# Cutting the mixed columns at 0, 136 and 648: one bank to route by, two of output

## The chip, the cores and the metric

The kernel runs on one core of a Trainium2 chip. The metric is the device time in microseconds, the median of several executions. A core has a matrix engine (TensorE, PE in the rows; its weight loads are listed apart as PEld), a vector engine (VectorE, DVE), a scalar engine (ScalarE, ACT), GpSimd (POOL), and queues that issue transfers (SyncE, SP). Matrix products land in PSUM, which has eight banks of 512 fp32 columns per partition.

## The reference, cut to what matters

Shapes: x is 128 samples of 64 channels by 1024; the output has the same shape.

```
h     = gelu(gelu(cond @ W0 + b0) @ W1 + b1)
att   = softmax(h @ W2 + b2)                              # 8 kernels per sample
y     = einsum('boi,bih->boh', att-weighted kernels, x) + bias   # mixes the 64 channels
logits= y @ W_router.T                                    # 8 experts
w     = top 2 of softmax(logits), renormalized
h_e   = einsum('nd,erd->ner', y, A)                       # rank 16, 8 experts
out   = x + y @ W_base.T + b_base + 2 * einsum('ner,eor->no', h_e * w, B)
```

## The kernel before, in words

Mixing the channels and multiplying by the wide matrix commute, so the kernel first multiplies the raw x by one matrix of 1160 columns, in this order: 128 columns of `A` (experts by rank), 8 of the router (together `AR` = 136), and 1024 of `W_base`. It calls the product z. Then it mixes: a 128x128 matrix that holds two samples' channel mixers is multiplied with z. The first 136 mixed columns are what a token is routed by; the other 1024 are output.

Rows come in 64 tiles of 128 (two samples each), two tiles to a unit, 32 units. The large product of a unit is a 2x2 block product done in seven products instead of eight (`A11`, `A12`, `S2`, `S1`, `S3`, `S4`, `A22`, where the S are sums of blocks that VectorE makes). Each product is made of matmuls of 290 columns, in two parts of twelve. fp32 accuracy comes from a split into a high and a low fp32r part: every product is three matmuls, high by high, high by low and low by high. ScalarE makes the high part by a cast, VectorE the low part by a subtraction, and so for x, for z (four blocks: z11 and z12 of the unit's first tile, z21 and z22 of the second), for the mixers and for the routed rows.

Behind the product each tile has two passes on TensorE:

- the mixed pass (`mixed`, lines 474 to 504): 3 pieces of columns, cut by `CUTS` at 0, 384 and 772, three matmuls each, into banks 4, 5 and 6. Piece 0 holds the 136 columns to route by and the first 248 of the output; its last matmul releases the routing on VectorE (`route`). Piece 1 first waits for the low part of z12 (or z22) and for `rest_put`.
- the experts' pass (`experts`, lines 506 to 518): the weighted, transposed rows `hwT` (high and low) by `b_hi` and `b_lo`, added to the output columns that stand in the same banks. With the cuts as they are that is 248, 388 and 388 columns, three times.

Then VectorE adds the tile's banks to `x_sb`, which already holds bias and x (`result`, two instructions), and SyncE stores it. Before the next tile's mixed pass ScalarE writes the tile's column bias into the banks (`seed`: piece 0 when `head_out` says that VectorE has read it, pieces 1 and 2 on `out_done`), so that the mixed pass accumulates on it.

The order of the work on each engine is written out by hand in `unit`, once per engine, with semaphores between. For unit u TensorE does: A11, A12, S2, experts of tile (u-1, 0), S1, mixed of (u-1, 1), S3, S4, experts of (u-1, 1), A22, mixed of (u, 0). VectorE's order in unit 1 is apart (`unit_1`); the last unit is written out too, with `expert_piece` and `add_piece` per piece and the last tile's stores cut in two.

Of the kernel before, what the change touches and what calls it, by code (L numbers as in the profile page):

```python
# [23 lines left out]
BANK = 512  # L24
# [5 lines left out]
XBLOCK = CHUNKS * P  # L30
WBLOCK = CHUNKS * HALF

CUTS = (0, 384, 772, WIDE)
PIECES = 3
LORA_SCALE = 2.0
ROUTE_STEPS = 9

# [58 lines left out]

def out_columns(piece):

    first = max(CUTS[piece], AR)
    return slice(first - AR, CUTS[piece + 1] - AR), slice(first - CUTS[piece], CUTS[piece + 1] - CUTS[piece])  # L100


def build(nc, x, xT, small, keep, mix_w, wide, b_base, bT, out):
# [8 lines left out]
    with ExitStack() as ctx:  # L112
# [117 lines left out]
        tile_bias_done = sem("tile_bias_done")  # L230
        head_put = sem("head_put")
        rest_put = sem("rest_put")
        head_out = sem("head_out")
        mix_hi_done = sem("mix_hi_done")
        mix_lo_done = sem("mix_lo_done")
        product_mm = sem("product_mm")
# [115 lines left out]
        @block.sync  # L352
        def _(sp):
            def load_mix(u, side):
                pair = agg_w_pairs[tile_no(u, side)]
                for par in range(PAIR):
                    blk = slice(par * CH, (par + 1) * CH)
                    sp.dma_start(mix[blk, side, blk], pair[blk, :]).then_inc(mix_in[side], 16)

            def load_first_mix(side):  # L360
                for par in range(PAIR):
                    b, blk = side * PAIR + par, slice(par * CH, (par + 1) * CH)
                    sp.dma_start(mix[blk, side, blk], agg_w[b:b + 1, :].rearrange("b (i o) -> b i o", i=CH)
                                 ).then_inc(mix_in[side], 16)

            def load_xT(u):
                sp.dma_start(xT_sb[:].rearrange("p b n -> p (b n)"), xT_units[u]).then_inc(xT_in, 16)

            def store(u, side):
                sp.wait_ge(out_done, tile_no(u, side) + 1)  # L370
                sp.dma_start(out_tiles[tile_no(u, side)], x_sb[:, side, :]).then_inc(stored[side], 16)

            def load_first(name):
                at = RAW[name]
                sp.dma_start(xT_sb[:, at, :], xT_units[0][:, at * XBLOCK:(at + 1) * XBLOCK]  # L375
                             ).then_inc(first_xT_in[at], 16)

            load_first("A11")
            for c in range(CHUNKS):
                cols = slice(c * HALF, (c + 1) * HALF)  # L380
                sp.dma_start(w_stage[:, 0, cols], wide_blocks[0][:, cols]).then_inc(b11_in[c], 16)  # L381
            load_first("A21")
            sp.dma_start(small_sb[:], small).then_inc(small_in, 16)
            load_first("A12")
            for h, js in enumerate(HALVES):
                cols = slice(js.start * HALF, js.stop * HALF)
                sp.dma_start(w_stage[:, 1, cols], wide_blocks[2][:, cols]).then_inc(b21_in[h], 16)
            load_first("A22")
            for h, js in enumerate(HALVES):
                cols = slice(js.start * HALF, js.stop * HALF)  # L390
                sp.dma_start(b12_sb[:, cols], wide_blocks[1][:, cols]).then_inc(b12_in[h], 16)
            for h, js in enumerate(HALVES):
                cols = slice(js.start * HALF, js.stop * HALF)
                sp.dma_start(b22_sb[:, cols], wide_blocks[3][:, cols]).then_inc(b22_in[h], 16)
            sp.wait_ge(x_lo_done, FIRST_SPLITS)
            load_xT(1)
            sp.wait_ge(zeroed, 2)
            sp.wait_ge(agg_done, 2 * GROUPS)
            load_first_mix(0)
            load_first_mix(1)  # L400
            sp.dma_start(agg_w_dram.rearrange("(b i) o -> b (i o)", b=BATCH), agg_w[:]).then_inc(agg_w_out, 16)
            sp.dma_start(bias_out[:], b_base.partition_broadcast(P)).then_inc(bias_out_in, 16)
            for side in range(2):
                sp.wait_ge(mix_in[side], 16 * PAIR)
            sp.wait_ge(agg_w_out, 16)
            sp.dma_start(bT_stage, bT).then_inc(bT_in, 16)
            sp.wait_ge(mix_lo_done, 2)
            load_mix(1, 0)
            load_mix(1, 1)

            def unit(u, par, first=False, early=False):
                store(u - 1, 0)
                sp.wait_ge(mix_lo_done, tile_no(u, 0) + 1)
                load_mix(u + 1, 0)
                sp.wait_ge(x_lo_done, splits(u, "A22"))
                load_xT(u + 1)
                store(u - 1, 1)
                sp.wait_ge(mix_lo_done, tile_no(u, 1) + 1)
                load_mix(u + 1, 1)

            units(sp, unit)
            store(LAST - 1, 0)
            store(LAST - 1, 1)
            sp.wait_ge(out_done, tile_no(LAST, 0) + 1)
            sp.dma_start(out_tiles[tile_no(LAST, 0)], last_x[:, 0, :]).then_inc(stored[0], 16)
            last_cols = [slice(0, out_columns(1)[0].stop), out_columns(2)[0]]
            for n, cols in enumerate(last_cols):
                sp.wait_ge(out_done, tile_no(LAST, 1) + 1 + n)
                sp.dma_start(out_tiles[tile_no(LAST, 1)][:, cols], last_x[:, 1, cols]).then_inc(stored[1], 16)
            sp.wait_ge(stored[0], UNITS * 16)  # L430
            sp.wait_ge(stored[1], UNITS * 16 + 16)

        @block.tensor
        def _(pe):
# [69 lines left out]
                mixed(1, 2, start=not seeded).then_inc(mixed_mm, 1)  # L504

            def expert_part(stat, mov, banks):
                for k in range(PIECES):
                    res, at = out_columns(k)
                    mm = nc.tensor.matmul(ps[:, banks[k], at], stat[:], mov[:, res], start=False, stop=True,  # L509
                                          skip_group_check=True)  # L510
                return mm

# [6 lines left out]

            def expert_piece(side, k, bank, start=False):  # L520

                res, at = out_columns(k)
                dst = ps[:, bank, at]
                pe.wait_ge(hwT_hi_done, tile_no(LAST, side) + 1)
                nc.tensor.matmul(dst, hwT_hi[:], b_hi[:, res], start=start, stop=False, skip_group_check=True)
                nc.tensor.matmul(dst, hwT_hi[:], b_lo[:, res], start=False, stop=False, skip_group_check=True)
                pe.wait_ge(hwT_lo_done, tile_no(LAST, side) + 1)
                return nc.tensor.matmul(dst, hwT_lo[:], b_hi[:, res], start=False, stop=True, skip_group_check=True)
# [172 lines left out]
                product_part(b, "S4", part, False).then_inc(last_half_mm, 1)  # L701
            pe.wait_ge(z22_lo_done, u + 1)
            mixed(1, 1, LAST_BANKS[1], last_z_hi, last_z_lo)
            expert_piece(0, 0, O_BANKS[0]).then_inc(last_piece_mm, 1)
            expert_piece(0, 1, O_BANKS[1], True)
            expert_piece(0, 2, O_BANKS[2], True)
            pe.wait_ge(last_half_summed, 1)
# [3 lines left out]
            mixed(0, 1, start=False).then_inc(last_piece_mm, 1)  # L711
            pe.wait_ge(last_half_lo_done, 2)
            mixed(0, 2, start=False).then_inc(last_piece_mm, 1)
            for k in range(PIECES):
                expert_piece(1, k, LAST_BANKS[k]).then_inc(last_piece_mm, 1)

        @block.scalar
        def _(act):
# [31 lines left out]
            def seed(u, side):  # L750

                t = tile_no(u, side)
                act.wait_ge(tile_bias_done, t - 1)
                act.wait_ge(head_out, t)
                nc.scalar.activation(ps[:, O_BANK, 0:width(0)], col_sum[:, columns(0)], ACT.Copy,
                                     scale=tile_bias[:, side:side + 1]).then_inc(head_put, 1)
                act.wait_ge(out_done, t)
# [261 lines left out]
        def _(dve):  # L1019
# [93 lines left out]
            def result(u, side):  # L1113
                t = tile_no(u, side)
                dve.wait_ge(x_in[side], u * 16 + 16)
                dve.wait_ge(out_mm, t + 1)
                res, at = out_columns(0)
                nc.vector.tensor_tensor(x_sb[:, side, res], ps[:, O_BANK, at], x_sb[:, side, res], ALU.add
                                        ).then_inc(head_out, 1)
                rest = x_sb[:, side, res.stop:D].rearrange("p (k n) -> p k n", k=2)  # L1120
                nc.vector.tensor_tensor(rest, ps[:, O_BANK + 1:O_BANK + 3, out_columns(1)[1]], rest,  # L1121
                                        ALU.add).then_inc(out_done, 1)

            def put_biases(u, side, place=x_sb):

# [71 lines left out]
            def unit_1():  # L1197
# [30 lines left out]
                dve.wait_ge(product_mm, products(1, "S4"))  # L1228
                add_acc(sum2, b, z12_summed)
                result(0, 1)  # L1230
                make_s3(2)
                x_low(2, "A11")
                z12_low(1)
                x_low(2, "A12")
                dve.wait_ge(x_lo_done, splits(2, "A11"))
                make_s2(2)
# [99 lines left out]
            hwT_low(u, 1)  # L1336

            def add_piece(side, k, bank):
                dve.wait_ge(last_piece_mm, side * PIECES + k + 1)
                res, at = out_columns(k)  # L1340
                return nc.vector.tensor_tensor(last_x[:, side, res], ps[:, bank, at], last_x[:, side, res], ALU.add)  # L1341

            dve.wait_ge(x_in[0], u * 16 + 16)
            add_piece(0, 0, O_BANKS[0])
            add_piece(0, 1, O_BANKS[1])
            add_piece(0, 2, O_BANKS[2]).then_inc(out_done, 1)
            dve.wait_ge(x_in[1], u * 16 + 16)
            add_piece(1, 0, LAST_BANKS[0])
            add_piece(1, 1, LAST_BANKS[1]).then_inc(out_done, 1)
            add_piece(1, 2, LAST_BANKS[2]).then_inc(out_done, 1)  # L1350

# [45 lines left out]
```

## Time and profile before

| what | value |
|---|---|
| median of 3 runs | 944.49 us (944.46 to 944.65) |
| the profiled execution | 944.94 us |
| its span, first to last instruction | 943.3 us |
| TensorE busy | 936.6 us, 99% |
| VectorE busy | 773.8 us, 82% |
| ScalarE busy | 476.4 us, 51% |
| granted TensorE clock | 1.00 of full speed |

The span lies inside the execution's own time, which is 1.64 us longer. A matmul's duration in the rows is from its start to its modelled end and overlaps that of the next one; what a matmul costs in a full queue is the distance between the starts of two neighbours. Rows of the timeline merge neighbouring instructions of one kind (x3), and then give the time from the first start to the last end.

### The profile page before, as it was taken

Reading aid. Unit: us, or ns where it says so; the run is one execution under the profiler, and the core shown is the slowest. Engines: PE = TensorE matmul, PEld = TensorE weight load, DVE = VectorE, ACT = ScalarE, POOL = GpSimd, SP = SyncE. Lnnn points to the kernel's source line nnn. Section 1 sums busy time; section 2 is a strip of 40 time slices with the busy share of each in tenths; the row PEclk is TensorE's granted clock in tenths of the full one; section 3 lists DMA queues with packets and bytes.
Section 4 is the critical chain, followed back from the end, with each engine's and each line's share of the span. In section 5 each row is a group of like instructions: output and inputs, shape, how many; then the busy total and the mean of one; then the engine's idle time right before and its main releaser. Section 6 shows DMA issues by size and latency. Waiting matters only on the chain.

```text
span 943.3 us, 19762 instructions
## 1 busy us (share of the span) xinstructions
PE 936.6 (99%) x6687; PEld 932.7 (99%) x6687; DVE 773.8 (82%) x2327; ACT 476.4 (51%) x915; POOL 97.5 (10%) x139
## 2 busy tenths in 40 slices
PE   9999999999999999999999999999999999999998
PEld 8999999999999999999999999999999999999997
DVE  5986666888888888888888888888888888888876
ACT  6655454545454455454454555454545454545451
POOL 1130101100101100101010101001011001011010
PEclk9999999999999999999999999999999999999999
DMA  8444435343445343444344354444353434453434
GB/s 300 149 109 103 108 116 137 95 133 90 104 127 134 92 127 79 114 134 115 111 112 92 114 136 105 122 95 110 114 136 97 129 91 107 120 136 93 134 91 112
DMA packets 36055, 111.41 MB, mean 118 GB/s; under 512 B 13200, under 2 KB 13456, under 8 KB 31936
## 3 DMA queue, kind: packets, MB, share of 16 engines
q1 hardware_dynamic: 26656, 77.32, 22.5%
q0 software_dynamic: 9376, 33.78, 21.9%
q8 instruction: 14, 0.23, 0.1%
q14 instruction: 9, 0.07, 0.0%
HBM read 75.37 MB, written 35.65 MB: 118 GB/s over the span
## 4 chain that ended last, share of the span: by engine, by line
PE 97%; DMA 1%; DVE 1%; SPq 0%; issue 0%; ACT 0%; DVEq 0%
PE ps L446 25%; PE ps L444 25%; PE ps L442 25%; PE ps L509 9%; PE ps L478 4%; PE ps L476 4%; PE ps L480 4%; DMA w_stage<-in_wide 1%; PE ps L469 0%; PE ps L468 0%; PE ps L535 0%; DVE w_stage L1341 0%; SPq L381 0%; SPq L375 0%; DVE w_lo L1133 0%
## 5 line engine op out<-in xcount | busy, mean ns | idle before, releaser
L442 PE MATMUL ps<-w_hi,x_hi 128*128 128x290 f32 x1544 | 457.9, 297 | 0.4 <-DVE x_lo L1138 0.3
L446 PE MATMUL ps<-w_hi,x_lo 128*128 128x290 f32 x1544 | 458.0, 297 | 0.0
L444 PE MATMUL ps<-w_lo,x_hi 128*128 128x290 f32 x1544 | 457.8, 296 | 0.0
L442 PEld LDWEIGHTS ps<-w_hi,x_hi 128*128 128x128 f32 x1544 | 292.0, 189 | 2.4 <-DVE w_lo L1133 0.9
L444 PEld LDWEIGHTS ps<-w_lo,x_hi 128*128 128x128 f32 x1544 | 291.4, 189 | 0.0
L446 PEld LDWEIGHTS ps<-w_hi,x_lo 128*128 128x128 f32 x1544 | 291.1, 189 | 0.0
L1107 DVE STREAM_TRANSPOSE blocks_hwT<-hw 32x32 f32<-32x32 f32 x832 | 168.5, 203 | 25.3
L720 ACT CAST x_hi<-xT_sb 128x512 fp32r<-128x512 f32 x186 | 112.5, 620 | 29.9 <-DVE xT_sb L1038 22.2
L1022 DVE TENSOR_TENSOR x_lo<-xT_sb,x_hi 128x512 fp32r<-128x512 f32 x186 | 125.1, 686 | 0.7 <-ACT x_hi L720 0.7
L763 ACT COPY sum<-ps 128x580 f32<-128x580 f32 x96 | 62.0, 646 | 111.4 <-PE ps L446 111.4
L993 POOL DMA_DIRECT2D x_sb<-in_x x62 | 53.7, 867 | 510.5 <-ACT x_sb L744 495.0
L739 ACT CAST hwT_hi<-blocks_hwT 128x128 fp32r<-128x128 f32 x52 | 15.6, 299 | 144.7 <-DVE blocks_hwT L1107 144.7
L988 POOL TENSOR_TENSOR mix_lo<-mix,mix_hi 128x128 fp32r<-128x128 f32 x64 | 47.7, 746 | 302.8 <-ACT mix_hi L724 302.8
L1041 DVE TENSOR_TENSOR sum<-ps,sum 128x580 f32<-128x580 f32 x91 | 68.8, 756 | 7.5 <-PE ps L446 7.4
L446 PE MATMUL ps<-t_hi,x_lo 128*128 128x290 f32 x248 | 74.2, 299 | 0.0
L442 PE MATMUL ps<-t_hi,x_hi 128*128 128x290 f32 x248 | 74.2, 299 | 0.0
L444 PE MATMUL ps<-t_lo,x_hi 128*128 128x290 f32 x248 | 73.9, 298 | 0.0
L476 PE MATMUL ps<-z_hi,mix_hi 128*128 128x384 f32 x189 | 64.0, 339 | 0.3 <-DVE z_lo L1050 0.3
L478 PE MATMUL ps<-z_hi,mix_lo 128*128 128x384 f32 x189 | 63.9, 338 | 0.0
L480 PE MATMUL ps<-z_lo,mix_hi 128*128 128x384 f32 x189 | 63.8, 338 | 0.0
L744 ACT COPY x_sb<-bias_out 128x1024 f32<-128x1024 f32 x60 | 62.8, 1046 | 0.0
L1121 DVE TENSOR_TENSOR x_sb<-ps,x_sb 128x776 f32<-128x776 f32 x62 | 59.2, 956 | 0.0
(137 smaller groups left out, 1232.3 us busy)
## 6 DMA issues: line engine op xcount, KB each, us to landing
xT_sb<-in_xT SPq DMA_DIRECT2D x31, 1024.0 KB, 4.9
x_sb<-in_x POOLq DMA_DIRECT2D x62, 512.0 KB, 5.4
result<-x_sb SPq DMA_DIRECT2D x62, 512.0 KB, 2.7
b_sb<-in_wide SPq DMA_DIRECT2D x4, 580.0 KB, 13.6
agg_w_rows<-agg_w SPq DMA_DIRECT2D x1, 2048.0 KB, 7.5
mix<-agg_w_rows SPq DMA_DIRECT2D x124, 16.0 KB, 2.5
w_stage<-in_wide SPq DMA_DIRECT2D x4, 290.0 KB, 5.3
w_stage<-in_wide SPq DMA_DIRECT2D x2, 580.0 KB, 8.3
```

The lines of the kernel that those rows point to most:

```text
L442: nc.tensor.matmul(dst, x_hi[:, s, rows], high[:, c, cols], start=first, stop=False, skip_group_check=True)
L444: nc.tensor.matmul(dst, x_hi[:, s, rows], low[:, c, cols], start=False, stop=False, skip_group_check=True)
L446: mm = nc.tensor.matmul(dst, x_lo[:, s, rows], high[:, c, cols], start=False, stop=last, skip_group_check=True)
L476: nc.tensor.matmul(dst, mix_hi[:, side, :], high[:, columns(k)], start=start, stop=False, skip_group_check=True)
L478: nc.tensor.matmul(dst, mix_lo[:, side, :], high[:, columns(k)], start=False, stop=False, skip_group_check=True)
L480: return nc.tensor.matmul(dst, mix_hi[:, side, :], low[:, columns(k)], start=False, stop=True, skip_group_check=True)
L509: mm = nc.tensor.matmul(ps[:, banks[k], at], stat[:], mov[:, res], start=False, stop=True, skip_group_check=True)
L720: nc.scalar.copy(x_hi[:, SLOT[name], :], raw(name)).then_inc(x_hi_done, 1)
L744: nc.scalar.copy(x_sb[:, side, :], bias_out[:]).then_inc(out_bias_put, 1)
L1022: nc.vector.tensor_tensor(x_lo[:, SLOT[name], :], raw(name), x_hi[:, SLOT[name], :].bitcast(F32), ALU.subtract).then_inc(x_lo_done, 1)
L1041: nc.vector.tensor_tensor(dst[:], acc(first), dst[:], ALU.add).then_inc(done, 1)
L1107: nc.vector.transpose(blocks_hwT[there, here], hw[here, there]).then_inc(blocks_made, 1)
```

## The change: new cuts, two output pieces

The cuts move from 0, 384, 772 to 0, 136, 648. Piece 0 is then exactly the 136 columns to route by; pieces 1 and 2 are a full bank of output each. The experts' pass touches only pieces 1 and 2, with 512 columns each. `result` becomes one instruction over both banks, and the semaphore `head_out` goes: the seed of piece 0 waits for `hw_done` (the routing has read bank 4). In the last unit one `expert_piece` and one addition per tile go, and the last tile is stored as two halves of 512 columns. In unit 1, `z12_low` moves up by two places on VectorE.

```diff
-CUTS = (0, 384, 772, WIDE)
-PIECES = 3
+CUTS = (0, AR, AR + BANK, WIDE)
+OUT_PIECES = (1, 2)
...
 def out_columns(piece):
-    first = max(CUTS[piece], AR)
-    return slice(first - AR, CUTS[piece + 1] - AR), slice(first - CUTS[piece], CUTS[piece + 1] - CUTS[piece])
+    return slice(CUTS[piece] - AR, CUTS[piece + 1] - AR)
...
             def expert_part(stat, mov, banks):
-                for k in range(PIECES):
-                    res, at = out_columns(k)
-                    mm = nc.tensor.matmul(ps[:, banks[k], at], stat[:], mov[:, res], start=False, stop=True,
+                for k in OUT_PIECES:
+                    mm = nc.tensor.matmul(ps[:, banks[k], :], stat[:], mov[:, out_columns(k)], start=False, stop=True,
                                           skip_group_check=True)
...
-            expert_piece(0, 0, O_BANKS[0]).then_inc(last_piece_mm, 1)
             expert_piece(0, 1, O_BANKS[1], True)
...
-            for k in range(PIECES):
+            for k in OUT_PIECES:
                 expert_piece(1, k, LAST_BANKS[k]).then_inc(last_piece_mm, 1)
...
                 act.wait_ge(tile_bias_done, t - 1)
-                act.wait_ge(head_out, t)
+                act.wait_ge(hw_done, t)
...
-                nc.vector.tensor_tensor(x_sb[:, side, res], ps[:, O_BANK, at], x_sb[:, side, res], ALU.add
-                                        ).then_inc(head_out, 1)
-                rest = x_sb[:, side, res.stop:D].rearrange("p (k n) -> p k n", k=2)
-                nc.vector.tensor_tensor(rest, ps[:, O_BANK + 1:O_BANK + 3, out_columns(1)[1]], rest,
-                                        ALU.add).then_inc(out_done, 1)
+                out = x_sb[:, side, :].rearrange("p (k n) -> p k n", k=2)
+                nc.vector.tensor_tensor(out, ps[:, O_BANK + 1:O_BANK + 3, :], out, ALU.add).then_inc(out_done, 1)
...
                 result(0, 1)
+                z12_low(1)
                 make_s3(2)
                 x_low(2, "A11")
-                z12_low(1)
                 x_low(2, "A12")
...
-            add_piece(0, 0, O_BANKS[0])
             add_piece(0, 1, O_BANKS[1])
...
-            add_piece(1, 0, LAST_BANKS[0])
             add_piece(1, 1, LAST_BANKS[1]).then_inc(out_done, 1)
```

TensorE's mixed pass of a tile stood before as follows (`z_hi`, `z_lo` the split product, `mix_hi`, `mix_lo` the split mixer):

```order
L476 MATMUL ps<-z_hi,mix_hi 128x384
L478 MATMUL ps<-z_hi,mix_lo 128x384
L480 MATMUL ps<-z_lo,mix_hi 128x384
L476 MATMUL ps<-z_hi,mix_hi 128x388
L478 MATMUL ps<-z_hi,mix_lo 128x388
L480 MATMUL ps<-z_lo,mix_hi 128x388
```

and stands now:

```order
L475 MATMUL ps<-z_hi,mix_hi 128x136
L477 MATMUL ps<-z_hi,mix_lo 128x136
L479 MATMUL ps<-z_lo,mix_hi 128x136
L475 MATMUL ps<-z_hi,mix_hi 128x512
L477 MATMUL ps<-z_hi,mix_lo 128x512
L479 MATMUL ps<-z_lo,mix_hi 128x512
```

Three more like the last three follow in each. The number of matmuls is the same, nine, and their columns add up to the same 1160.

The experts' pass, also on TensorE, behind product S2 (and again behind S4), before:

```order
L509 MATMUL ps<-b_hi,hwT_hi 128x248
L509 MATMUL ps<-b_hi,hwT_hi 128x388 x2
L509 MATMUL ps<-b_lo,hwT_hi 128x248
L509 MATMUL ps<-b_lo,hwT_hi 128x388 x2
L509 MATMUL ps<-b_hi,hwT_lo 128x248
L509 MATMUL ps<-b_hi,hwT_lo 128x388 x2
```

and now:

```order
L445 MATMUL ps<-w_hi,x_lo 128x290
L507 MATMUL ps<-b_hi,hwT_hi 128x512 x2
L507 MATMUL ps<-b_lo,hwT_hi 128x512 x2
L507 MATMUL ps<-b_hi,hwT_lo 128x512 x2
L441 MATMUL ps<-w_hi,x_hi 128x290
```

Nine matmuls have become six, over the same columns.

VectorE at the end of unit 1, from the sum that completes z12 on (`sum`; `x_sb<-ps` is `result`, `z_lo<-sum` the low part of z12, the rest makes the next unit's x blocks), before:

```order
L1041 TENSOR_TENSOR sum<-ps,sum 128x580
L1118 TENSOR_TENSOR x_sb<-ps,x_sb 128x248
L1121 TENSOR_TENSOR x_sb<-ps,x_sb 128x776
L1030 TENSOR_TENSOR xT_sb<-xT_sb 128x512
L1022 TENSOR_TENSOR x_lo<-xT_sb,x_hi 128x512
L1050 TENSOR_TENSOR z_lo<-sum,z_hi 128x580
```

and now:

```order
L1038 TENSOR_TENSOR sum<-ps,sum 128x580
L1115 TENSOR_TENSOR x_sb<-ps,x_sb 128x1024
L1047 TENSOR_TENSOR z_lo<-sum,z_hi 128x580
L1027 TENSOR_TENSOR xT_sb<-xT_sb 128x512
L1019 TENSOR_TENSOR x_lo<-xT_sb,x_hi 128x512 x2
```

The z12 split has moved ahead of S3 and of the low part of `A11`, in this unit alone; the merged `result` is in every unit.

## Rows read from the trace of the kernel before

**Rows 1.** The page, its busy times, granted clock and chain of waits.
```profile
PE 936.6 (99%) x6687; PEld 932.7 (99%) x6687; DVE 773.8 (82%) x2327; ACT 476.4 (51%) x915; POOL 97.5 (10%) x139
...
PEclk9999999999999999999999999999999999999999
...
PE 97%; DMA 1%; DVE 1%; SPq 0%; issue 0%; ACT 0%; DVEq 0%
```

**Rows 2.** Waits of TensorE: who waited for whom, total us, times, longest.
```profile
PE ps L476 <- DVE z_lo L1050: 0.3, 1, 0.3
```

**Rows 3.** Timeline of PE, 500 to 506 us: start us, us, engine, line, operation.
```profile
499.97 0.64 PE L509 MATMUL ps<-b_hi,hwT_hi 128*128 128x248 f32 x3
...
501.37 0.30 PE L442 MATMUL ps<-w_hi,x_hi 128*128 128x290 f32 x1
...
503.00 0.30 PE L442 MATMUL ps<-w_hi,x_hi 128*128 128x290 f32 x1
...
504.21 0.29 PE L442 MATMUL ps<-w_hi,x_hi 128*128 128x290 f32 x1
...
504.61 0.34 PE L476 MATMUL ps<-z_hi,mix_hi 128*128 128x384 f32 x1
...
505.13 0.34 PE L476 MATMUL ps<-z_hi,mix_hi 128*128 128x388 f32 x1
...
506.02 0.33 PE L480 MATMUL ps<-z_lo,mix_hi 128*128 128x388 f32 x1
506.19 0.30 PE L442 MATMUL ps<-w_hi,x_hi 128*128 128x290 f32 x1
```

**Rows 4.** Timeline of PE, 15 to 16 us: two matmuls of 8 columns.
```profile
15.29 0.28 PE L535 MATMUL ps<-small_sb,h2T 128*128 128x8 f32 x2
```

**Rows 5.** The same two by line: durations in ns, min/median/max.
```profile
L535 PE MATMUL ps<-small_sb,h2T x2: 172/214/256, 15.3 to 15.3; 128*128 128x8 f32 x2
```

**Rows 6.** Timeline of PEld, 15.4 to 15.85 us.
```profile
15.67 0.19 PEld L442 LDWEIGHTS ps<-w_hi,x_hi 128*128 128x128 f32 x1 [0.19 <-DVE w_lo L1133]
15.78 0.19 PEld L444 LDWEIGHTS ps<-w_lo,x_hi 128*128 128x128 f32 x1
```

**Rows 7.** Timeline of PE, 53 to 54 us.
```profile
53.43 0.27 PE L532 MATMUL ps<-keep_sb,hw 128*128 128x128 f32 x1
...
53.67 0.30 PE L444 MATMUL ps<-w_lo,x_hi 128*128 128x290 f32 x1
```

**Rows 8.** Timeline of all engines in unit 1, 75.9 to 77.1 us.
```profile
75.93 0.77 DVE L1050 TENSOR_TENSOR z_lo<-sum,z_hi 128x580 fp32r<-128x580 f32 x1
...
76.11 0.34 PE L480 MATMUL ps<-z_lo,mix_hi 128*128 128x384 f32 x1
...
76.74 0.19 PEld L476 LDWEIGHTS ps<-z_hi,mix_hi 128*128 128x128 f32 x1 [0.61 <-DVE z_lo L1050]
...
77.03 0.34 PE L478 MATMUL ps<-z_hi,mix_lo 128*128 128x388 f32 x1
```

**Rows 9.** Timeline of all engines, 501.5 to 505.2 us.
```profile
501.64 0.42 DVE L1118 TENSOR_TENSOR x_sb<-ps,x_sb 128x248 f32<-128x248 f32 x1 [0.47 <-PE ps L509]
...
501.97 0.96 DVE L1121 TENSOR_TENSOR x_sb<-ps,x_sb 128x776 f32<-128x776 f32 x1
...
502.84 0.68 DVE L1030 TENSOR_TENSOR xT_sb<-xT_sb 128x512 f32<-128x512 f32 x1
502.96 0.91 ACT L758 ACTIVATE ps<-col_sum,tile_bias 128x776 f32<-128x776 f32 x1
...
504.04 0.76 DVE L1050 TENSOR_TENSOR z_lo<-sum,z_hi 128x580 fp32r<-128x580 f32 x1
...
504.96 0.19 PEld L476 LDWEIGHTS ps<-z_hi,mix_hi 128*128 128x128 f32 x1
```

**Rows 10.** Line 1341, the last additions: ns min/median/max.
```profile
L1341 DVE TENSOR_TENSOR w_stage<-ps,w_stage x6: 406/553/553, 936.9 to 938.9; 128x388 f32<-128x388 f32 x4, 128x248 f32<-128x248 f32 x2
```

**Rows 11.** DMA issues, 936 to 943.5 us: KB each, us to landing.
```profile
result<-w_stage SPq DMA_DIRECT2D x1, 194.0 KB, 3.3
```

More of the change, by code:

```diff
@@ L232, in build @@
         rest_put = sem("rest_put")
-        head_out = sem("head_out")
         mix_hi_done = sem("mix_hi_done")
@@ L425, in _ @@
             sp.dma_start(out_tiles[tile_no(LAST, 0)], last_x[:, 0, :]).then_inc(stored[0], 16)
-            last_cols = [slice(0, out_columns(1)[0].stop), out_columns(2)[0]]
-            for n, cols in enumerate(last_cols):
+            for n, k in enumerate(OUT_PIECES):
+                cols = out_columns(k)
                 sp.wait_ge(out_done, tile_no(LAST, 1) + 1 + n)
@@ L520, in expert_piece @@
             def expert_piece(side, k, bank, start=False):
-                res, at = out_columns(k)
-                dst = ps[:, bank, at]
+                res = out_columns(k)
+                dst = ps[:, bank, :]
                 pe.wait_ge(hwT_hi_done, tile_no(LAST, side) + 1)
@@ L1116, in result @@
                 dve.wait_ge(out_mm, t + 1)
-                res, at = out_columns(0)
-                nc.vector.tensor_tensor(x_sb[:, side, res], ps[:, O_BANK, at], x_sb[:, side, res], ALU.add
-                                        ).then_inc(head_out, 1)
-                rest = x_sb[:, side, res.stop:D].rearrange("p (k n) -> p k n", k=2)
-                nc.vector.tensor_tensor(rest, ps[:, O_BANK + 1:O_BANK + 3, out_columns(1)[1]], rest,
-                                        ALU.add).then_inc(out_done, 1)
+                out = x_sb[:, side, :].rearrange("p (k n) -> p k n", k=2)
+                nc.vector.tensor_tensor(out, ps[:, O_BANK + 1:O_BANK + 3, :], out, ALU.add).then_inc(out_done, 1)
             def put_biases(u, side, place=x_sb):
@@ L1338, in add_piece @@
             def add_piece(side, k, bank):
-                dve.wait_ge(last_piece_mm, side * PIECES + k + 1)
-                res, at = out_columns(k)
-                return nc.vector.tensor_tensor(last_x[:, side, res], ps[:, bank, at], last_x[:, side, res], ALU.add)
+                dve.wait_ge(last_piece_mm, side * len(OUT_PIECES) + k)
+                res = out_columns(k)
+                return nc.vector.tensor_tensor(last_x[:, side, res], ps[:, bank, :], last_x[:, side, res], ALU.add)
             dve.wait_ge(x_in[0], u * 16 + 16)
-            add_piece(0, 0, O_BANKS[0])
             add_piece(0, 1, O_BANKS[1])
```

## The prediction

> **What bounds the kernel now.** I read the page first. TensorE is busy 99% of the span, the chain of waits runs through it for 97%, and its granted clock is full throughout, the level of 2.4 GHz [rows 1]. Then the waits of TensorE: beyond the start there is one, 0.3 us, on a z split of line 1050 [rows 2]. So every nanosecond that a matmul takes in a full queue is paid, and what VectorE and ScalarE save is worth nothing unless TensorE waits. The timeline then gives what a matmul costs, as the distance between starts [rows 3]:
>
> - 290 columns: nine from 503.00 to 504.21, 0.134 us each.
> - 388 columns: five from 505.13 to 506.02, 0.178 us each.
> - a whole mixed pass: 504.61 to 506.19, about 1.585 us with the rounding (1.58 to 1.59).
> - a whole experts' pass: 499.97 to 501.37, 1.40 us. Six matmuls of 388 are 1.07 of it, which leaves 0.11 for one of 248.
>
> **What a matmul of 136 columns costs.** Nothing in the trace has this shape in a full queue, and the change hangs on it: 192 matmuls (3 in each of 64 tiles) will have it. From 290 to 388 columns the cost grows by 0.044 us for 98, so by columns alone 136 would take 0.134 - 154 x 0.00044 = 0.067 us. But each matmul has its own load of 128x128 weights, and three places show what a load costs when nothing hides it.
>
> - Two matmuls of 8 columns take 0.28 us from the first start to the last end [rows 4]; the shorter, which is the first, takes 172 ns [rows 5]. Their own work is the same, so the second ends 0.11 us behind the first, for 8 columns: it had to wait for its weights.
> - A fresh load of a block of x (fp32r, as the weights here are), the queue empty before it, starts at 15.67, and the next load, which starts when the matmul of the first does, at 15.78: 0.11 us [rows 6].
> - A transposition of 128 columns and the matmul of 290 behind it take 53.43 to 53.67, 0.24 us [rows 7]; less the usual 0.134 that is 0.11 for the 128.
>
> The load of the next matmul runs under the present one, and only that one. A matmul of 248 columns or more covers it; one of 136 can't. I take 0.112 us, bounds 0.108 and 0.114 (the 248 columns' share, which may itself be the load).
>
> The Trainium skill gives for the same thing, in "TensorE: Matmul & The Clock Gate", section "Back-to-back issue gap", about 81 ns for N=128 in a stream of loads and matmuls, and about 131 ns for N=512. The trace speaks against the second figure: 388 columns already take 0.178. By the first the 192 matmuls would cost 192 x 0.031 = 6.0 us less than in my sum, an outcome of its own below.
>
> **What a matmul of 512 columns costs.** From 388 on, at one column per cycle of 2.4 GHz: 0.178 + 124/2400 = 0.229. With the slope between 290 and 388 it is 0.178 + 0.055 = 0.232. I take 0.230; lower end 0.228, upper 0.232.
>
> **The sum, part by part.**
>
> 1. Mixed pass: 3 x 0.112 + 6 x 0.230 = 1.716 against 1.585, +0.131 per tile, 64 tiles: +8.4 us. Three matmuls fall from 0.173 to 0.112 (504.61 to 505.13 was 0.52 for three), not to the 0.067 of their columns, while the six others pay for all the columns moved to them.
> 2. Experts' pass: 6 x 0.230 = 1.38 against 1.40, -0.02 per tile: -1.3 us. Three matmuls fewer, but the same columns, and it is the columns that were paid.
> 3. Unit 1: from 76.11 to 77.03 are 0.92 us, where two matmuls take 0.35 [rows 8]: 0.57 us of stall, a late split and the uncovered load behind it. Moved up two instructions of VectorE, each about 0.60 from start to start, the split ends well before 76.1. What is late next there is the low part of `A11`, made 0.67 later, for a product that starts behind the mixed pass: no wait. -0.6 us.
> 4. `result` as one instruction: before 0.33 + 0.87 = 1.20 us from start to start [rows 9]; by the slope of these two, 0.54 for 528 columns, 1024 take 1.12. VectorE gains 0.08 per tile, worth nothing by itself, but see the second rival.
> 5. Seeds on ScalarE: piece 0 gets shorter and earlier, pieces 1 and 2 go from 776 columns (0.91) to 1024, by columns about 1.1. They start when `result` ends, about 502.9, so end near 504.0, and the mixed matmul that needs them starts after 504.8. Hidden, with 0.7 us to spare. Without this cover each 0.1 us late would cost 6 us over the tiles.
> 6. The tail: what ends last is the last addition and the last store. The addition is of 512 columns instead of 388 (0.553 us [rows 10], by the slope above +0.13), its matmul some 0.05 longer behind its start, and the last store 256 KB instead of 194 [rows 11], of two that hold 512 KB together as before; I put 0.05 on it. +0.2 us. The routing of the last tiles, released 0.18 earlier by the shorter piece 0, isn't what the tail waits for.
>
> Together +8.4 - 1.3 - 0.6 + 0.2 = +6.7 us on the profiled execution's 944.94, so 951.6. The median of the runs before is 0.45 below that execution, and so is the forecast: **951.2 us**. Its own range: the 0.002 on the 12 matmuls of 512 is 1.5 us either way, the bounds of the 136 give -0.8 and +0.4. That is 949.0 to 953.1.
>
> **The rivals.**
>
> - *Columns are all that counts: faster.* The loads are pipelined deeper than one, so 136 columns cost 0.067. For it: a load is listed with 0.19 us [rows 6] and one starts with every matmul, each 0.134, so loads overlap already. Against it: the two matmuls of 8 columns, 0.11 apart. Price: 192 x 0.045 = 8.6 us less, 942.6. It decides from a cost of 0.077 on: below that the pass costs less than it saves. Chance 0.05. The Trainium skill's isolated gap of N/2.4 + 2.5 ns (same page and section as above) is this rule in its purest form; the 290 columns would take 0.123 by it and the trace has 0.134.
> - *A load partly hidden: no change.* The load of the next matmul begins before the present one starts, so that a third of the uncovered 0.045 is left, 0.082 us for a short matmul. For it: nothing but the overlap of the listed loads. Against it: all three places show 0.11. Price: 192 x 0.030 = 5.8 us less than the forecast, 945.4. Chance 0.04. The 81 ns of the Trainium skill, cited above, would be this, and 945.2.
> - *A new wait: slower still.* Piece 1 now comes 3 x 0.112 after the start of the pass instead of 0.52, and its load one matmul earlier, at +0.22 where it was at +0.35 (504.96 against 504.61 [rows 9]). It waits for the z12 split, which ends at 504.80, +0.19, and releases the load some 0.04 later (in unit 1 the split ends at 76.70 and the load starts at 76.74 [rows 8]). With VectorE's 0.08 it is released at about +0.15, so 0.07 to spare. If the merged `result` gains nothing, the two meet; from there every 0.1 us costs 31 x 0.1 = 3.1 us. With 0.1 that makes 954.3. Chance 0.07.
> - *My forecast*, the short matmul bound by its load and no new wait: 0.84.
>
> **How the numbers follow.** The profile bears the forecast's mechanism in three places and no place speaks for less, hence the weight. The range that should hold the time 8 times in 10 is the forecast's own with a little of the third rival: 948.8 to 953.6. A difference of less than 0.2%, 1.9 us, is about what a measurement can't tell from none. Faster takes the first rival, 0.05. The second is no change, 0.04. Slower takes the forecast and the third, 0.91.
>
> **What would show it.** In the profile after, the starts of matmuls of 136 columns lie 0.11 apart and those of 512 columns 0.23; if the first are at 0.07 or 0.08, step 1 is wrong and so is the sign. A mixed pass takes 1.72 us and an experts' pass 1.38. TensorE has no wait on the z12 split, in unit 1 or later; a wait of that name with 30 entries is the third rival. VectorE's busy time falls by about 5 us with no effect. TensorE stays at 99% busy, since a short matmul that waits for its weights is listed as busy.

## The result: 7.1 us slower

| | before | changed |
|---|---|---|
| median, first measurement | 944.57 us (4 runs) | 951.66 us (4 runs, 951.05 to 951.90) |
| span of the profiled execution | 943.3 us | 949.4 us |
| TensorE busy | 936.6 us | 943.8 us |
| matmuls in the trace | 6687 | 6495 |

The ratio is 1.0074, with a 95% interval from 1.0056 to 1.0091. The forecast was 951.2 us, range 948.8 to 953.6.

The page after: TensorE still holds the chain at full clock, with 192 matmuls fewer and 7 us more of busy time; the busy share of its weight loads has fallen [rows 1].

```profile
PE 943.8 (99%) x6495; PEld 907.3 (96%) x6495; DVE 773.0 (81%) x2263; ACT 475.8 (50%) x915; POOL 97.5 (10%) x139
...
PEclk9999999999999999999999999999999999999999
...
PE 98%; DMA 1%; DVE 0%; SPq 0%; ACT 0%; issue 0%; DVEq 0%
```

The timeline of TensorE after, an experts' pass, the product behind it and a mixed pass, the same place in the program as [rows 3]:

```profile
502.80 0.63 PE L507 MATMUL ps<-b_hi,hwT_hi 128*128 128x512 f32 x2
...
504.19 0.29 PE L441 MATMUL ps<-w_hi,x_hi 128*128 128x290 f32 x1
...
507.39 0.23 PE L475 MATMUL ps<-z_hi,mix_hi 128*128 128x136 f32 x1
507.46 0.27 PE L477 MATMUL ps<-z_hi,mix_lo 128*128 128x136 f32 x1
507.57 0.28 PE L479 MATMUL ps<-z_lo,mix_hi 128*128 128x136 f32 x1
507.68 0.44 PE L475 MATMUL ps<-z_hi,mix_hi 128*128 128x512 f32 x1
507.96 0.40 PE L477 MATMUL ps<-z_hi,mix_lo 128*128 128x512 f32 x1
...
508.89 0.39 PE L479 MATMUL ps<-z_lo,mix_hi 128*128 128x512 f32 x1
509.12 0.29 PE L441 MATMUL ps<-w_hi,x_hi 128*128 128x290 f32 x1
```

The mixed pass takes 507.39 to 509.12, 1.73 us, where it took 1.58. Over all passes of the two traces the medians are 1.725 and 1.584. The experts' pass takes 502.80 to 504.19, 1.39, where it took 1.40. A matmul of 512 columns costs (508.89 - 507.96) / 4 = 0.2325 at this place and 1.39 / 6 = 0.232 in the experts' pass. The listed starts of the short matmuls mislead: the second stands 0.07 behind the first, but its duration has grown from 0.23 to 0.27, and the first of the long ones has 0.44 instead of 0.39. So part of a listed duration is waiting. The loads are the better guide: a load starts when the matmul in front of it does, here at 507.39 and again at 507.96. The weight loads at the same place:

```profile
507.39 0.19 PEld L477 LDWEIGHTS ps<-z_hi,mix_lo 128*128 128x128 f32 x1
507.50 0.19 PEld L479 LDWEIGHTS ps<-z_lo,mix_hi 128*128 128x128 f32 x1
507.62 0.19 PEld L475 LDWEIGHTS ps<-z_hi,mix_hi 128*128 128x128 f32 x1
507.73 0.19 PEld L477 LDWEIGHTS ps<-z_hi,mix_lo 128*128 128x128 f32 x1
507.96 0.19 PEld L479 LDWEIGHTS ps<-z_lo,mix_hi 128*128 128x128 f32 x1
```

These are 0.11 us apart for 136 columns, four starts over three matmuls, then 0.23 for 512. The loss grows evenly. The mixed pass of [rows 3] began 2.78 us later after the change (507.39 against 504.61). Thirteen units earlier it began 0.31 us sooner:

```profile
133.49 0.23 PE L475 MATMUL ps<-z_hi,mix_hi 128*128 128x136 f32 x1
```

where the kernel before has

```profile
133.80 0.34 PE L476 MATMUL ps<-z_hi,mix_hi 128*128 128x384 f32 x1
```

That is 3.09 us in 13 units, 0.238 per unit or 0.119 per tile, 7.6 us if it held for all 64.

The early lead has two parts. The first mixed pass of all began 0.41 us sooner in this execution (46.63 against 47.03), before any pass that the change cuts anew; over the fourteen traces of all runs that start lies between 46.55 and 47.27 with no order by kernel, so it is scatter. And the stall of unit 1 [rows 8], 0.57 us, is missing. The two add up to the 1.0 us by which the spans' difference of 6.1 falls short of the medians' 7.1.

### The profile page after: what moved, and what is told of

Its sections match the earlier page's. It is cut to its first block, busy times and chain, and to the rows that moved or that the text cites. A ratio compares the mean times of both kernels' runs of the same rounds, so it can differ in the third digit from the quotient of the medians.

```text
span 949.4 us, 19314 instructions
## 1 busy us (share of the span) xinstructions
PE 943.8 (99%) x6495; PEld 907.3 (96%) x6495; DVE 773.0 (81%) x2263; ACT 475.8 (50%) x915; POOL 97.5 (10%) x139
## 4 chain that ended last, share of the span: by engine, by line
PE 98%; DMA 1%; DVE 0%; SPq 0%; ACT 0%; issue 0%; DVEq 0%
PE ps L445 25%; PE ps L443 25%; PE ps L441 25%; PE ps L507 9%; PE ps L477 4%; PE ps L479 4%; PE ps L475 4%; DMA w_stage<-in_wide 1%; PE ps L468 0%; PE ps L467 0%; DVE w_stage L1334 0%; PE ps L533 0%; SPq L380 0%; SPq L374 0%; DVE w_lo L1126 0%; PE ps L530 0%
## 5 line engine op out<-in xcount | busy, mean ns | idle before, releaser
L1115 DVE TENSOR_TENSOR x_sb<-ps,x_sb 128x1024 f32<-128x1024 f32 x62 | 75.9, 1224 | 32.5 <-PE ps L507 29.9
L755 ACT ACTIVATE ps<-col_sum,tile_bias 128x1024 f32<-128x1024 f32 x60 | 66.9, 1116 | 18.2 <-DVE x_sb L1115 18.2
L477 PE MATMUL ps<-z_hi,mix_lo 128*128 128x136 f32 x189 | 67.3, 356 | 0.0
L479 PE MATMUL ps<-z_lo,mix_hi 128*128 128x136 f32 x189 | 67.1, 355 | 0.0
L475 PE MATMUL ps<-z_hi,mix_hi 128*128 128x136 f32 x189 | 66.8, 353 | 0.0
```

The source lines that it names most:

```text
L475: nc.tensor.matmul(dst, mix_hi[:, side, :], high[:, columns(k)], start=start, stop=False, skip_group_check=True)
L477: nc.tensor.matmul(dst, mix_lo[:, side, :], high[:, columns(k)], start=False, stop=False, skip_group_check=True)
L479: return nc.tensor.matmul(dst, mix_hi[:, side, :], low[:, columns(k)], start=False, stop=True, skip_group_check=True)
L1115: nc.vector.tensor_tensor(out, ps[:, O_BANK + 1:O_BANK + 3, :], out, ALU.add).then_inc(out_done, 1)
```

## The experiments

Twelve further measurements were made, each beside the kernel before on the same chip. Its median differs by up to 0.2 us from one group of runs to the next, so a difference between two rows with another "before there" is uncertain by as much.

| run | median us | before there |
|---|---|---|
| e1 changed kernel again | 951.77 | 944.70 |
| e2 changed, old place of the z12 split | 951.70 | 944.70 |
| e3 changed, piece 0 padded to 248 columns | 952.00 | 944.70 |
| e4 before, z12 split early, store in halves | 943.68 | 944.70 |
| e5 before, z12 split early | 944.45 | 944.52 |
| e6 before, cuts at 264 and 712 | 954.47 | 944.52 |
| e7 changed, `result` in two | 953.09 | 944.52 |
| e8 changed, one load less | 948.30 | 944.52 |
| e9 as e8, z12 split early in every unit | 945.10 | 944.59 |
| e10 as e7, z12 split early in every unit | 951.38 | 944.59 |
| e11 before, last store cut at 624 | 944.15 | 944.59 |
| e12 before, last store in halves | 943.94 | 944.59 |

### Is it the load or the columns?

**e1**, the reference: 

> The changed kernel again, as the reference point for the runs beside it on the same chip. Both theories: 951.7 us, 7.1 above before.

It took 951.77, ratio 1.0075 (1.0061 to 1.0089).

**e3** gives the short matmuls more to do:

```diff
-                dst = ps[:, O_BANK + k if bank is None else bank, 0:width(k)]
+                size = width(k) if k else 248
+                cols = slice(CUTS[k], CUTS[k] + size)
+                dst = ps[:, O_BANK + k if bank is None else bank, 0:size]
```

and `cols` for `columns(k)` in the three matmuls. 

> The changed kernel, but the three matmuls of piece 0 in each mixed pass stream 248 columns instead of 136; the 112 extra columns go into unread places of bank 4. Theory (a short matmul costs its 128x128 weight load, 0.112 us, whatever its columns): 248 columns cost 0.114, so 192 x 0.002 = +0.4 us, 952.1. Rival (columns are what is paid and the loss comes from elsewhere, as from full banks of 512): 112 columns x 0.00044 = 0.049 us each, 192 of them, +9.4 us, 961.

952.00, 0.23 above e1, as the theory has it. The 112 columns more in each of 192 matmuls cost next to nothing. The timeline of TensorE in e3 shows the same spacing, 0.11 to 0.12 us, now with even durations:

```profile
507.75 0.28 PE L477 MATMUL ps<-z_hi,mix_hi 128*128 128x248 f32 x1
507.86 0.28 PE L479 MATMUL ps<-z_hi,mix_lo 128*128 128x248 f32 x1
507.98 0.28 PE L481 MATMUL ps<-z_lo,mix_hi 128*128 128x248 f32 x1
508.09 0.40 PE L477 MATMUL ps<-z_hi,mix_hi 128*128 128x512 f32 x1
```

**e6** puts the short matmul into the other pass, with no matmul of 512 columns in either:

```diff
-CUTS = (0, 384, 772, WIDE)
+CUTS = (0, 264, 712, WIDE)
```

> The kernel before with its cuts at 0, 264 and 712: the mixed pass has pieces of 264, 448 and 448 columns, the experts' pass of 128, 448 and 448. No matmul has 512 columns and the mixed pass has no short one, but the experts' pass has three. Theory (a short matmul costs its load, 0.112): experts 3 x 0.112 + 6 x 0.2045 = 1.563 against 1.404, mixed 3 x 0.123 + 6 x 0.2045 = 1.596 against 1.586, together +0.169 in each of 64 tiles, +10.8 us, 955.3; perhaps 0.2 more for the stall in unit 1. Rival (the loss comes with full banks of 512, columns are what is paid): 128 columns cost 0.063, +0.022 per tile, +1.4 us, 946.

954.47, ratio 1.0108 (1.0092 to 1.0123), 9.95 us above before and 0.8 short of the expected 955.3. The rival's 946 is out. The experts' pass in e6:

```profile
504.12 0.68 PE L509 MATMUL ps<-b_hi,hwT_hi 128*128 128x128 f32 x3
504.64 0.68 PE L509 MATMUL ps<-b_lo,hwT_hi 128*128 128x128 f32 x3
505.16 0.68 PE L509 MATMUL ps<-b_hi,hwT_lo 128*128 128x128 f32 x3
505.68 0.29 PE L442 MATMUL ps<-w_hi,x_hi 128*128 128x290 f32 x1
```

That is 0.52 us for each three and 1.56 at this rounding (1.553 over all such passes), against 1.40: the same 1024 columns three times, 0.15 dearer.

**e8** takes one load away and keeps the columns:

```diff
+                if k == 0:
+                    wide_dst = ps[:, O_BANK if bank is None else bank, 0:2 * AR]
+                    nc.tensor.matmul(wide_dst, mix_hi[:, side, :], high[:, 0:2 * AR], start=start, stop=False,
+                                     skip_group_check=True)
+                    return nc.tensor.matmul(dst, mix_lo[:, side, :], high[:, columns(0)], start=False, stop=True,
+                                            skip_group_check=True)
```

> The changed kernel, but piece 0 of a mixed pass has two matmuls instead of three: mix_hi by 272 columns of z_hi (136 of them into unread places) and mix_lo by 136. The product with z_lo is left out of the columns to route by, as it would be if z_hi and z_lo stood side by side and were streamed as one. The number of columns streamed is the same, 408. Theory (one load fewer that nothing covers): 0.126 + 0.112 = 0.238 against 0.336, -0.098 in 64 tiles, -6.3 us, 945.4. Rival (columns): 0.126 + 0.067 = 0.193 against 0.201, -0.5 us, 951.2.

948.30, 3.5 below e1, between the theory's -6.3 and the rival's -0.5. The timeline of e8 tells why. A mixed pass of a unit's first tile, with the z12 split ahead of it:

```profile
505.02 0.76 DVE L1053 TENSOR_TENSOR z_lo<-sum,z_hi 128x580 fp32r<-128x580 f32 x1
...
505.61 0.29 PE L477 MATMUL ps<-z_hi,mix_hi 128*128 128x272 f32 x1
...
505.74 0.22 PE L479 MATMUL ps<-z_hi,mix_lo 128*128 128x136 f32 x1
505.82 0.19 PEld L481 LDWEIGHTS ps<-z_hi,mix_hi 128*128 128x128 f32 x1
```

and one of a second tile, whose z22 is long split:

```profile
521.59 0.29 PE L477 MATMUL ps<-z_hi,mix_hi 128*128 128x272 f32 x1
...
521.72 0.23 PE L479 MATMUL ps<-z_hi,mix_lo 128*128 128x136 f32 x1
521.72 0.19 PEld L481 LDWEIGHTS ps<-z_hi,mix_hi 128*128 128x128 f32 x1
```

The first load of piece 1 stands 0.21 behind the start of the pass in the one and 0.13 in the other. The split ends at 505.78 and the load follows 0.04 later, as in unit 1 of the kernel before [rows 8]. The pass got so short that the wait of the prediction's third rival came true here, though the list of TensorE's waits shows nothing of it: the matmul in front is listed as busy meanwhile.

**e9** moves the split ahead in every unit:

```diff
                 result(u - 1, 1)
+                z12_low(u)
                 make_s3(u + 1)
                 x_low(u + 1, "A11")
-                z12_low(u)
```

> The kernel with one load less in piece 0 (the product with z_lo left out of the columns to route by), and the z12 split moved ahead of S3 and of the low part of A11 on VectorE in every unit, not in unit 1 alone. Where only one load was taken away the mixed passes took 1.631 us where the split is older, and 1.716 where they wait for z12, 0.085 more. Theory (that difference is the wait for the split, the rest is the load): both kinds take 1.63, -0.085 x 30 = -2.5 us, 945.8. Rival (that difference is not the split): 948.3.

945.10: 3.2 less than e8, and 6.7 below e1. The closest partner is e10 below, which stood beside it, has the early split too and keeps all three matmuls (and has `result` in two, which costs it nothing): 951.38, 6.3 more, which is just what one load of 0.098 in 64 passes gives. That is the third side from which the columns are excluded. Its mixed pass, of a first tile too, takes 504.82 to 506.44, 1.62 us. Against before it is no change that can be told (ratio 1.0007, 0.9997 to 1.0016), and it leaves part of the routing's precision out, so it is no better kernel.

What e3, e6 and e9 exclude is that columns alone are paid. In all of them every matmul brings its own load of 128x128, and none changes the size of a load. A floor of 0.11 us on each pair of load and matmul, from another cause than the weights, would fit them as well; that it is the load itself is argued and not shown.

### How near is the wait for the z12 split?

In the changed kernel the split ends at 507.56, and the load of piece 1 starts 0.06 behind it, at 507.62:

```profile
504.46 1.22 DVE L1115 TENSOR_TENSOR x_sb<-ps,x_sb 128x1024 f32<-128x1024 f32 x1 [0.70 <-PE ps L507]
505.60 0.68 DVE L1027 TENSOR_TENSOR xT_sb<-xT_sb 128x512 f32<-128x512 f32 x1
...
506.80 0.76 DVE L1047 TENSOR_TENSOR z_lo<-sum,z_hi 128x580 fp32r<-128x580 f32 x1
```

**e7** makes VectorE a little slower ahead of the split:

```diff
-                out = x_sb[:, side, :].rearrange("p (k n) -> p k n", k=2)
-                nc.vector.tensor_tensor(out, ps[:, O_BANK + 1:O_BANK + 3, :], out, ALU.add).then_inc(out_done, 1)
+                for k in OUT_PIECES:
+                    cols = out_columns(k)
+                    add = nc.vector.tensor_tensor(x_sb[:, side, cols], ps[:, O_BANK + k, :], x_sb[:, side, cols],
+                                                  ALU.add)
+                add.then_inc(out_done, 1)
```

> The changed kernel with result as two instructions of VectorE again, 512 columns each. Theory (TensorE pays for matmuls and their loads alone; the z12 split is released just in time): VectorE loses about 0.06 us per tile, the split is released at the moment at which the load of piece 1 wants it; 0 to 0.05 us in each of 31 units, 951.7 to 953.2. Rival (the new wait already costs time after the change, so VectorE's time is TensorE's): +0.06 x 31 = +1.9 us or more, 953.6.

953.09, 1.4 us above the changed kernel, at the upper end of the theory. In e7 the split ends at 508.71 and the load starts at 508.76, 0.17 behind the one before it, where the changed kernel has 0.11 to 0.12:

```profile
507.95 0.76 DVE L1047 TENSOR_TENSOR z_lo<-sum,z_hi 128x580 fp32r<-128x580 f32 x1
...
508.59 0.19 PEld L479 LDWEIGHTS ps<-z_lo,mix_hi 128*128 128x128 f32 x1
...
508.76 0.19 PEld L475 LDWEIGHTS ps<-z_hi,mix_hi 128*128 128x128 f32 x1
```

**e10** is e7 with e9's move. 

> The changed kernel with result in two instructions again, and the z12 split ahead of S3 and of the low part of A11 in every unit. With the two instructions alone, the mixed passes that wait for z12 took 1.778 us instead of 1.723, and the time was 1.4 us above the changed kernel. Theory (a late split): with the split early these passes take 1.725 again and the time is that of the changed kernel, 951.7. Rival (VectorE's two reads of the banks slow TensorE in another way): 953.1.

951.38, 1.7 below e7: the wait was the split's, and with the split early VectorE's second instruction costs nothing. It is also 0.3 to 0.4 below the changed kernel, too little for these runs to tell.

### Unit 1

**e5** has this move alone on the kernel before:

```diff
                 result(0, 1)
+                z12_low(1)
                 make_s3(2)
                 x_low(2, "A11")
-                z12_low(1)
```

> The kernel before with the z12 split of unit 1 moved up, and nothing else of the change. Theory: TensorE's 0.57 us of stall in unit 1 go, 944.0. Rival (absorbed later): 944.5.

944.45 against 944.52, ratio 1.0001 (0.9992 to 1.0010). The medians speak for the rival, but the interval is 0.9 us wide to either side and doesn't exclude a gain of 0.5. **e2** is the changed kernel with the move undone, the same four lines the other way. 

> The changed kernel with the z12 split of unit 1 back in its old place on VectorE. Theory (the stall in unit 1 is real and the move removes it): the first load of piece 1 stands 0.22 us after the start of the mixed pass instead of 0.35, and the merged result gains 0.06, so TensorE stalls about 0.57 + 0.13 - 0.06 = 0.64 us in unit 1 and nowhere else; +0.6 us against the changed kernel, 952.3. Rival (something later in unit 1 absorbs it): +0.0.

951.70 against e1's 951.77, five executions each, all within 951.4 to 952.0: no sign of the 0.6. The loads of unit 1 in e5 show a stall in spite of the move, in another place:

```profile
75.59 0.19 PEld L476 LDWEIGHTS ps<-z_hi,mix_hi 128*128 128x128 f32 x1 [0.26 <-issue]
75.70 0.19 PEld L478 LDWEIGHTS ps<-z_hi,mix_lo 128*128 128x128 f32 x1
75.88 0.19 PEld L480 LDWEIGHTS ps<-z_lo,mix_hi 128*128 128x128 f32 x1
76.42 0.19 PEld L476 LDWEIGHTS ps<-z_hi,mix_hi 128*128 128x128 f32 x1 [0.36 <-issue]
```

and what ScalarE and VectorE did there:

```profile
72.40 0.69 DVE L1026 TENSOR_TENSOR s_sb<-xT_sb 128x512 f32<-128x512 f32 x1 [1.87 <-DMA xT_sb<-in_xT]
...
74.90 0.58 ACT L755 ACTIVATE ps<-col_sum,tile_bias 128x384 f32<-128x384 f32 x1
75.42 0.89 ACT L758 ACTIVATE ps<-col_sum,tile_bias 128x776 f32<-128x776 f32 x1
```

The seeds end at 75.48 and 76.31, 0.11 us ahead of the two loads. The list gives no releaser for them, so that the seeds held them is read from these times. Everything here waits for unit 2's x, which VectorE got at 72.40 in this execution, at 71.95 in e2's (stall 0.2 on the split by its trace), at 72.14 in e1's (none) and at 71.26 in the changed kernel's first (none). When x is late, the seeds are next after the split. Two more traces, of kernels whose split is in its old place, show the same hold of x on the stall: e11 got x at 71.85 and its load waited 0.30, e12 at 72.21 and it waited 0.67.

### The tail

**e4** adds to e5's move

```diff
-            last_cols = [slice(0, out_columns(1)[0].stop), out_columns(2)[0]]
+            last_cols = [slice(0, D // 2), slice(D // 2, D)]
```

> The kernel before (cuts 0, 384, 772) with two small parts of the change: the z12 split of unit 1 moved up, and the last tile stored as two halves of 512 columns instead of 636 and 388. Theory: 0.57 us of stall go in unit 1; the last store landed 2.66 us behind its issue after the change and 3.34 before, and if the sizes are what did it, 0.5 go too, though the first half now waits for nothing else: 943.4 to 944.0. Rival (the landing is scatter, the stall is absorbed): 944.5, no change.

943.68 against 944.70, ratio 0.9990 (0.9981 to 0.9999): the one kernel below before with an interval clear of 1, by 1.0 us. **e12** has the halves alone. 

> The kernel before with the last tile stored in halves of 512 columns and nothing else. Theory (of the 1.0 us by which the kernel with both the early z12 split and the halves beat the one before, the halves gave what the stores' landing shows, and the split's share hangs on when the next unit's x arrives): -0.5 us, 944.0 where before has 944.5. Rival (the split gave it all): no change.

943.94 against 944.59, 0.65 less; its interval (0.9984 to 1.0002) includes no change. **e11** asks why, with `last_cols = [slice(0, 624), slice(624, D)]`. 

> The kernel before, with the last tile's two stores cut at column 624 instead of 636: rows of 2496 and 1600 bytes, both multiples of 64, where 636 gave 2544 and 1552. Before, the stores of the last unit took 4.60 us from the first issue to the last landing, and with halves of 2048 bytes 4.05. Theory (it is whether the rows begin and end on a multiple of 64 bytes): 4.05 to 4.1, 0.5 us less than before. Rival (it is the uneven sizes, or the short rows): 4.6, no change.

944.15, 0.44 less, in the noise (0.9988 to 1.0006). The landing is plainer than the time. The transfers of the last unit, in e11:

```profile
result<-w_stage SPq DMA_DIRECT2D x1, 312.0 KB, 2.7
result<-w_stage SPq DMA_DIRECT2D x1, 200.0 KB, 2.9
```

and in e4:

```profile
result<-w_stage SPq DMA_DIRECT2D x2, 256.0 KB, 2.7
```

against 3.3 for the last one before [rows 11]. From the first issue to the last landing that is 4.13 and 4.05 us against 4.60. e11 also made the last store 6 KB larger, but e6 speaks against the sizes. Its cuts give rows of 2304 and 1792 bytes, uneven and the last one short, and both multiples of 64:

```profile
result<-w_stage SPq DMA_DIRECT2D x1, 288.0 KB, 2.5
result<-w_stage SPq DMA_DIRECT2D x1, 224.0 KB, 2.5
```

So most of the half microsecond goes with rows that begin on a multiple of 64 bytes, and neither uneven nor short rows are needed for it. e6's last two stores were issued 0.61 us apart and not 0.47, as in the changed kernel, and there is one trace of each cut, except that the cut at 636 landed late in e5 too (3.2) and the halves early in every trace that has them.

## Why the prediction was right, step by step

- **The cost of a short matmul (step 1)**, the heart of it: 0.112 predicted, 0.11 in the loads' rows. e3, e6 and e9 each exclude the columns. The value read from two matmuls of 8 columns at the kernel's start [rows 4, 5] held for fp32r weights in a full queue. That the floor is the weights' load and not something else of each pair stays argued, as said above; the time is the same either way.
- **The cost of 512 columns** was mis-sized at the edge of its bounds: 0.230 taken, 0.232 measured. The continued slope was right, one column per cycle was not. So the mixed pass costs 0.142 more per tile instead of 0.131, and the experts' pass saves 0.010 instead of 0.020 (steps 1 and 2, means of a unit's two tiles in the middle of the traces). Together that is 8.4 us over 64 tiles where steps 1 and 2 add up to 7.1, so 1.3 us too little.
- **What the sum left out.** One product has become a little shorter: from the first matmul of A22 to the mixed pass 504.19 to 507.39, 3.20 us, against 501.37 to 504.61, 3.24 [rows 3]. The others hardly moved (A11 to S2 together 9.635 against 9.623). In a unit of the middle the passes give 0.264 us and the drift from unit to unit is 0.240, so the products took 0.024 back, 0.8 us over 32 units. The cause is open.
- **Unit 1 (step 3)**: the stall is gone in the traces of the changed kernel, but -0.6 was a figure of one execution. e2 and e5 show no such difference in the medians. The part that failed is that no wait is next once the split is moved up: when x arrives late, the seeds are late right behind the split, as in e5.
- **`result` and the seeds (steps 4 and 5)**: `result` takes 1.14 us from start to start (504.46 to 505.60), not 1.12. It had no effect by itself, as said. VectorE's busy time was to fall by 5 us and fell by 0.8; nothing hung on it, and its cause stays open.
- **The tail (step 6)** went the other way: +0.2 predicted. From the start of the last matmul to the end of the span were 4.8 us (938.44 to 943.3) and are 4.3 (945.13 to 949.4). The landing of the last store, put at +0.05, was the term mis-sized: it fell from 3.3 to 2.6. The forecast asked for its size alone and not for where its rows begin.
- **The third rival** did not strike, but by luck of 0.01 us, not with the 0.07 worked out. The split ends at 507.56 and the load starts 0.06 later; a load that waits for the split starts 0.05 behind its end (e7). VectorE gave 0.02 less than thought, and the product ahead of the pass was 0.03 to 0.04 shorter. e7, with some 0.06 more on VectorE, was enough for 1.4 us. The sign that the prediction named, a listed wait with 30 entries, was blind: e7 and e8 wait for the split in every unit and the list of waits has none of it.
- **The Trainium skill's figures.** In "TensorE: Matmul & The Clock Gate", section "Back-to-back issue gap", the Trainium skill gives 81 ns for 128 columns in a stream of loads and matmuls and 131 ns for 512. The runs have 0.11 us for 136 and 128 columns and 0.232 for 512, and the measurement decides. The same page of the Trainium skill, section "LDWEIGHTS (loading the stationary operand)", puts a load at P/1.2 ns for P columns, which gives an estimate of 107 ns for 128. The spacing of 0.11 agrees with it.
- **Two slips in the text.** Step 4 points to the second rival where it means the third, and the forecast's own range begins at 948.9 and not at 949.0 (951.2 less 1.5 and 0.8). Neither bears on the result.

The errors nearly cancel: +1.3 for the 512 columns and +0.6 for unit 1, less 0.8 for the shorter product and 0.7 for the tail, +0.4 in all, where 7.1 us were measured and 6.7 forecast. The time came within 0.5 us and the main term is shown. That the sum came closer than its smaller terms is luck.

## What to carry to other kernels

When every matmul brings its own 128x128 load of fp32r, as here, cut columns so that no piece falls below about 250. That is an estimate: the line through the costs of 290 and 388 columns meets 0.112 us at 240, and 248 columns cost 0.11 to 0.12 in e3. A shorter piece costs the same 0.11 whatever it has to do, and the columns moved out of it are paid in full where they go. Fewer matmuls are worth little by comparison: three fewer in the experts' pass, over the same columns, saved 0.01 us. And after shortening a pass, look at what its second piece waits for: a wait on a weight load hides in the busy time of the short matmul in front and isn't in the list of waits.

## What the runs showed of the hardware

- A matmul with its own load of 128x128 fp32r weights costs at least 0.11 us in a full queue at 2.4 GHz (136 columns in the changed kernel, 128 in e6, 0.114 to 0.119 for 248 in e3). A load starts when the matmul in front of it does. Between 290 and 512 columns a matmul costs 0.44 ns per column, (0.232 - 0.134) / 222, a little over one cycle.
- A store of rows of 1552 bytes landed in 3.2 to 3.3 us as the last of three, one of 1600 bytes in 2.9, one of 2048 in 2.6 to 2.7, one of 1792 in 2.5.
